# One gathered tile in 48 moves from GpSimd's indirect gather to SP's row-by-row copies

## What is computed

```python
N = emb.shape[0]
h = emb
acc = emb
for _ in range(LAYERS):
    h = jax.ops.segment_sum(adj_val[:, None] * h[adj_col], adj_row, num_segments=N)
    acc = acc + h
graph_item_embs = acc / (LAYERS + 1)
combined = graph_item_embs[items] + item_features[items]
...
scores = select @ _l2norm(graph_item_embs).T
```

## Time and profile before

| | us |
|---|---|
| median of 3 runs (lowest, highest) | 4309.99 (4309.81, 4310.87) |
| the profiled execution's own time | 4304.17 |
| its span in the profile | 4302.3 |
| sorting, until SP reads back the sorted lines | 0 to 738.3 |
| layer 0, GpSimd's first to last gather | 742.7 to 2302.0 |
| layer 1, GpSimd's first to last gather | 2334.4 to 3892.8 |
| GpSimd (POOL) busy in the whole span | 2982.2 (69%) |
| TensorE (PE) busy; VectorE (DVE) busy | 3380.7 (79%); 3127.0 (73%) |

### The profile page before, as it was taken

The page is one execution under the profiler, slowest core; times in us unless marked ns, Lnnn a source line. Parts: engine busy times, 40 slices in busy tenths (PEclk is TensorE's granted clock), DMA queues, the critical chain, the costliest instruction groups (busy, mean ns, idle before and its releaser), DMA issues. The chain is left out here.

```text
span 4302.3 us, 44283 instructions
## 1 busy us (share of the span) xinstructions
PE 3380.7 (79%) x9794; PEld 1811.7 (42%) x9794; DVE 3127.0 (73%) x7270; ACT 870.6 (20%) x3004; POOL 2982.2 (69%) x3071
## 2 busy tenths in 40 slices
PE   3899996787788877777876777777777777777888
PEld 2777774333333333333333333333333333334444
DVE  8999995777777777777775766667666776667555
ACT  0999996000000000000000000000000000007443
POOL 2477666777777777777775777777777777775760
PEclk8898887656665566666666767667676767766889
DMA  1000000221221221221125222222122221235693
GB/s 35 3 4 3 3 3 19 53 53 52 53 53 52 53 53 52 53 53 53 52 53 157 53 53 53 52 53 53 53 53 53 53 52 53 53 112 97 68 112 156
DMA packets 140407, 235.66 MB, mean 55 GB/s; under 512 B 56692, under 2 KB 84272, under 8 KB 140144
## 3 DMA queue, kind: packets, MB, share of 16 engines
q0 software_dynamic: 96288, 178.10, 19.1%
q1 hardware_dynamic: 41476, 55.61, 3.8%
q10 hardware_dynamic: 2508, 0.60, 0.1%
HBM read 193.16 MB, written 41.01 MB: 54 GB/s over the span
## 5 line engine op out<-in xcount | busy, mean ns | idle before, releaser
L1356 PE MATMUL bank<-ring 128*128 128x256 f32 x4992 | 2429.2, 604 | 692.5 <-DVE ring L1031 647.4
L1356 PEld LDWEIGHTS bank<-ring 128*128 128x128 f32 x4992 | 1120.9, 270 | 1977.5 <-DVE ring L1031 1941.4
L1031 DVE TENSOR_SCALAR ring<-bank,mlo,mval 128x256 f32<-128x256 f32 x2496 | 1353.2, 542 | 748.8 <-DMA ring<-table,cring 389.5
L516 POOL DMA_INDIRECT ring<-table,cring x1248 | 1178.5, 944 | 412.3 <-issue 379.9
L516 POOL DMA_INDIRECT ring<-in_L_rec_emb,cring x1248 | 1179.4, 945 | 384.4 <-issue 379.6
L1080 DVE TENSOR_TENSOR acc<-acc,bank 128x256 f32 x2496 | 1023.4, 410 | 172.1 <-issue 171.3
L602 ACT COPY mlo<-ring 128x24 f32 (+1 forms) x104 | 22.0, 211 | 2898.4 <-PE bank L1356 2895.4
L586 ACT ACTIVATE big<-big 128x68 f32<-128x68 bf16 x1764 | 558.0, 404 | 0.0
L1293 PE MATMUL bank<-big,ring 128*128 128x136 f32 x2352 | 441.3, 324 | 61.5 <-DVE ring L819 15.7
L486 POOL DMA_INDIRECT sorted_edges<-moved,block_to x313 | 399.7, 1277 | 101.9 <-issue 101.9
L1293 PEld LDWEIGHTS bank<-big,ring 128*128 128x128 f32 x2352 | 348.2, 211 | 152.7 <-ACT big L586 133.3
(11 more groups left out here) (209 smaller groups left out, 1620.7 us busy)
## 6 DMA issues: line engine op xcount, KB each, us to landing
scores<-stage SPq DMA_DIRECT2D x48, 512.0 KB, 2.6
ring<-in_L_rec_emb,cring POOLq DMA_INDIRECT x1248, 2.5
ring<-table,cring POOLq DMA_INDIRECT x1248, 2.5
table<-big SPq DMA_DIRECT2D x7, 896.0 KB, 8.4
combined<-ring SPq DMA_DIRECT2D x7, 896.0 KB, 7.5
sorted_edges<-moved,block_to POOLq DMA_INDIRECT x313
ring<-combined,sidi POOLq DMA_INDIRECT x200, 4.9
sorted_edges<-ring SPq DMA_DIRECT2D x1, 1248.0 KB, 4.4
```

The lines of the kernel that those rows point to most:

```text
L516: pool.indirect_dma_start(msg[:, s, :], None, source, bass.IndirectOffsetOnAxis(cring[:, s:s + 1], 0)).then_inc(s_g[s], 16)
L1031: dve.tensor_scalar(onehot[:, u % SR, :], bank[7][:, 0:BUCKET], mlo[:, u:u + 1], mval[:, u:u + 1], ALU.is_equal, ALU.mult).then_inc(s_S, 1)
L1356: pe.matmul(bank[u % PR][:, 0:BUCKET], msg[:, h * T + u, :], onehot[:, u % SR, :], start=True, stop=True).then_inc(s_mm[u % M], 1)
```

## The change

In both layers the last tile of each pair of rounds, slot 47 of `msg`, isn't gathered by GpSimd any more, except in the last pair. For the 25 other pairs SP copies its 128 rows one by one: SP loads 16 row numbers at a time into registers and issues 16 DMAs of one row each, with the source address from a register. The row numbers come from `own_col`, one partition wide, which DVE makes once from an extra read-back of the lines of these 25 tiles. SP starts on a pair's tile when the add of the same slot in the pair before is done (`s_acc[M - 1]`), waits for all 128 rows, clears their semaphore and raises `s_own_in`, for which DVE's one-hot of that slot waits. M becomes 4 in place of 6.

```diff
@@ constants @@
+    PAIRS = NST // 2 - 1
+    ROWS_AT_ONCE = 16
-    M = 6
+    M = 4
@@ semaphores @@
-        s_g = [sem(f"s_g{u}") for u in range(2 * T)]
+        s_g = [sem(f"s_g{u}") for u in range(2 * T - 1)]
@@ SP, behind the read-back of the sorted lines @@
+            sp.dma_start(own_lines.rearrange("o k s w -> o k (s w)"),
+                         lines[0:2 * T * PAIRS, :].rearrange("(k t) w -> t k w", t=2 * T)[2 * T - 1:2 * T]
+                         ).then_inc(s_lines, 16)
+
+            def last_of_pairs(layer, source):
+
+                sp.wait_ge(s_own, 2)
+                with sp.Fori(0, PAIRS) as i:
+                    sp.wait_ge(s_acc[M - 1], i * (2 * T // M) + (PER * layer + 1))
+                    for a in range(0, P, ROWS_AT_ONCE):
+                        _, cols = nc.values_load_multi_w_load_instructions(
+                            own_col[:, bass.ds(i * P + a, ROWS_AT_ONCE)], engines=[mybir.EngineType.SP],
+                            min_val=0, max_val=N - 1, skip_runtime_bounds_check_because=HELD)
+                        for p, col in enumerate(cols):
+                            sp.dma_start(msg[a + p:a + p + 1, 2 * T - 1, :], source[bass.ds(col, 1), :]).then_inc(s_one, 16)
+                    sp.wait_ge(s_one, 16 * P)
+                    sp.sem_clear(s_one)
+                    sp.sem_inc(s_own_in, 1)
+
+            last_of_pairs(0, emb)
@@ SP, behind the two loads of emb (413, 416 before) @@
+            last_of_pairs(1, table1)
@@ gather_step, GpSimd @@
-                for u in range(T):
+                for u in range(T if h == 0 or c == NST - 1 else T - 1):
@@
-                                            bass.IndirectOffsetOnAxis(cring[:, s:s + 1], 0)).then_inc(s_g[s], 16)
+                                            bass.IndirectOffsetOnAxis(cring[:, s:s + 1], 0)
+                                            ).then_inc(s_g[s] if s < 2 * T - 1 else s_late, 16)
@@ DVE, behind decode(T, NT, ...) @@
+            dve.wait_ge(s_lines, 16)
+            dve.tensor_copy(own_col.rearrange("o (k s) -> o k s", k=PAIRS), own_lines[:, :, :, 0]).then_inc(s_own, 1)
+            dve.wait_ge(s_own, 1)
+            dve.tensor_single_scalar(own_col, own_col, BUCKET.bit_length() - 1, ALU.arith_shift_right).then_inc(s_own, 1)
@@ one_hot, DVE @@
-                dve.wait_ge(s_g[u], 16 * ((NST // 2) * layer + it + 1))
+                if u < 2 * T - 1:
+                    dve.wait_ge(s_g[u], 16 * ((NST // 2) * layer + it + 1))
+                elif last:
+                    dve.wait_ge(s_late, 16 * (layer + 1))
+                else:
+                    dve.wait_ge(s_own_in, it + (PAIRS * layer + 1))
```

More of the change, by code:

```diff
@@ L93, in recommender_program @@
     TC = [T * (NST * n // 3) for n in range(4)]
+    HELD = "a column is held between 0 and N - 1, and an unused slot's is its tile's number, below NT <= N"
     FITS = "a tile's offset is 256 times the buckets that begin at or before it, less one: 0 to ROWS - 256"
@@ L151, in recommender_program @@
         sorted_rows = big[:, 0:-(-NT // P) * 2 * P].rearrange("p (m s w) -> p m s w", w=2, s=P)
+        at[0] = -(-NT // P) * 2 * P
+        own_lines = carve(big, PAIRS * 2 * P)[0:1, :].rearrange("o (k s w) -> o k s w", k=PAIRS, w=2)
+        assert at[0] <= ROWS
         at[0] = 0
@@ L209, in recommender_program @@
         block_at_l = carve(stage, NKL * P)
+        own_col = stage[0:1, 6 * D:6 * D + PAIRS * P].bitcast(I32)
+        assert 6 * D + PAIRS * P <= 4 * 512 * 2
         assert at[0] <= 4 * 512 * 2
@@ L317, in recommender_program @@
         s_iota = sem("s_iota")
-        s_g = [sem(f"s_g{u}") for u in range(2 * T)]
+        s_lines = sem("s_lines")
+        s_own = sem("s_own")
+        s_one = sem("s_one")
+        s_own_in = sem("s_own_in")
+        s_late = sem("s_late")
+        s_g = [sem(f"s_g{u}") for u in range(2 * T - 1)]
         s_S = sem("s_S")
@@ L1026, in _, with one_hot @@
             decode(T, NT, -(-NT // P))
-            def one_hot(layer, it, u):
-                dve.wait_ge(s_g[u], 16 * ((NST // 2) * layer + it + 1))
+            dve.wait_ge(s_lines, 16)
+            dve.tensor_copy(own_col.rearrange("o (k s) -> o k s", k=PAIRS), own_lines[:, :, :, 0]).then_inc(s_own, 1)
+            dve.wait_ge(s_own, 1)
+            dve.tensor_single_scalar(own_col, own_col, BUCKET.bit_length() - 1, ALU.arith_shift_right).then_inc(s_own, 1)
+            def one_hot(layer, it, u, last=False):
+                if u < 2 * T - 1:
[4 more added lines that the diff above has]
+                    dve.wait_ge(s_own_in, it + (PAIRS * layer + 1))
                 dve.tensor_scalar(onehot[:, u % SR, :], bank[7][:, 0:BUCKET], mlo[:, u:u + 1], mval[:, u:u + 1],
@@ L1084, in round_step @@
                     if not last or u + LEAD < T:
-                        one_hot(layer, it + (1 if h == 1 and u + LEAD >= T else 0), (h * T + u + LEAD) % (2 * T))
+                        one_hot(layer, it + (1 if h == 1 and u + LEAD >= T else 0), (h * T + u + LEAD) % (2 * T), last)
                 if layer == 0 and not (isinstance(c, int) and c >= L):
```

## The result

The changed kernel takes 4702.3 us (median of 4; 4694.1 to 4709.7) against 4309.9 before, a ratio of 1.0912 (95% interval 1.0898 to 1.0926). The forecast was slower, at 4442 us. The profiled execution took 4694.1 us.

What follows compares the result with a forecast made beforehand. GpSimd's gather step was taken as the bound; with SP setting the pace, layer 0 gains 61.2 us and layer 1 70.8, so 4304.2 + 132 = 4436, with 5.8 to the median 4442 us; 8-in-10 range 4238 to 4770.

Steps and rivals of the forecast that it cites:

- What bounds the kernel, and that SP takes over: Both layers run at GpSimd's gather step; SP's loop of 62.6 us a pair then sets the pace, against GpSimd's 58.7.
- G: Time from SP's release to its signal for one tile: 59.4 us, bounds 42 and 80.
- the issue: Issue of one single-row copy on SP: 0.29 us, between 0.17 and 0.42.
- register instruction and gaps: Per row on SP: one register instruction at 0.05 us and the gap between two issues at 0.045.
- A load of 16: SP's load of 16 row numbers into registers: 1.0 us, between 0.8 and 1.5; eight a tile, 8.0 us.
- The landing: SP's wait for its last row copy to land, with wait's end, clear and signal: 2.1 us a tile.
- The law of time over G: Each microsecond of G is worth 50 us; 56.8 gives no change, 55.5 or less gains the whole 62.5 us.
- Rival 1: SP keeps up and is hidden behind GpSimd, with a row at 0.355 us: 4248 us; chance 0.40.
- Rival 2: SP's issue costs 0.42 or 0.33 us, G 76 or 64.5: about 5270 or 4700 us; chance 0.20 above G = 64.
- Rival 3: SP's copies disturb GpSimd's gathers, step 1.28 us instead of 1.249: about 4323 us with SP hidden; chance 0.01.
- The loads' floor: Skill's floor of about 600 ns for SP's register loads: eight loads 4.8 us, G 56.2, time about 4282 us.
- Costed at nothing: Four semaphores, DVE's extra register instructions, the extra 25-row load, the moved features load and shared DMA engines were priced at zero.

Runs made afterwards that it cites:

- the 112-row run: Changed kernel with SP copying only rows 0 to 111 of its tiles, sums not the reference's: 4309.2 us beside 4307.4 for the kernel before.
- the split: Changed kernel with SP copying rows 0 to 95 and ACT rows 96 to 127: 4242.6 us against 4303.1 before; on the second kind of chip 6124 to 6203.
- 32-number loads: Changed kernel with 32 row numbers to a register load instead of 16: 4625.9 us against 4302.8 before; on the second kind of chip 6977 to 6995.

## Why the forecast had the sign and not the size

- *What bounds the kernel, and that SP takes over:* as forecast. DVE's wait for SP, GpSimd's wait for PE and SP without idle time were all named ahead.
- *The value of G:* the step that failed, a term that was mis-sized. The prediction said "G = 49.3 + 8.0 + 2.1 = 59.4 us". Measured: 51.7 + 10.1 + 1.0, and 1.3 in the slower rows, 64.1. By terms: the issue was put at 0.29 and took 0.22; register instruction and gaps were put at 0.095 and took 0.184, because a second register instruction stands there, and each of the three has a gap. The two errors nearly cancel, and leave + 2.4 us. A load of 16 was put at 1.0 and costs 1.26 with its surroundings, + 2.1; DVE's idle time of 1.53 us, from which it was scaled down, isn't what its load of 24 takes, which is 1.60 us. The landing was put 1.1 too high, and the slower rows weren't in the sum. Each microsecond counts 50 times, so 4.7 us are 235 of the 260 us missing; layer 1's dearer issues, 0.6 us in 25 pairs, are another 15.
- *The law of time over G,* "each microsecond of G is worth 50 us, G = 56.8 gives no change": right in three places. G = 56.8 gave 4309 us; G of 64.1 and 64.8 gives 4442 + 25 x (4.7 + 5.4) = 4695, measured 4702; SP hidden was to give 62.5 us and gave 60.5.
- *Rival 1,* SP keeps up, needed an issue of 0.26 us at the assumed gaps. The issue was even cheaper and the rival still failed, at the gaps and the loads. *Rival 2,* everything above G = 64, has the right time for a wrong reason: it wanted an issue of 0.33 or 0.42, and the issue took 0.22. Its 4700 is hit by chance. *Rival 3* is out on this kind of chip: GpSimd's gather takes 0.944 us with SP's copies and 0.945 without, and the 112-row run loses nothing.
- *The loads' floor.* The Trainium skill's "DMA: Bandwidth & Descriptors", section "Latency and other measured facts", gives a floor of about 600 ns. No load of these traces has fewer than 16 numbers, so they don't show it; from 1.14 us for 16 to 2.04 for 32 the number of registers decides. The same page says that the time to initiate a DMA is "usually small relative to the DMA itself" ("Issuing engines are not separate DMA queues"). For one copy the trace agrees, 0.22 us and at least 1.0 more to its landing; but 128 in a row are 28 us, and 51.7 with the instructions around them.
- *Costed at nothing:* four semaphores, the delayed start in layer 0 and the features load stayed free; the split contains all of them and comes within 2 us of the full gain. The jump back at the loop's end, 2.4 us, wasn't priced at all and is hidden in the 3.2 us.

## What to carry to other kernels

When work is moved from the engine that sets the pace to an idle one, compare the idle one's whole turn, with every small instruction, gap, load and landing, to the pace, and work out how much the total changes per unit of error; here 128 repeats and 50 turns turn 20 ns a row into 128 us. If the turn comes out near the limit, move less or share it: three quarters on SP and one quarter on ACT turned +9% into -1.4%. And a gain that rests on a queue of many short instructions should be measured on more than one chip.

## What the hardware showed that was not expected

- A DMA of one row with its address from a register is issued in 0.22 us on SP and on ACT, less than the 0.277 for 85 rows and 0.33 for 128. On SP it takes 0.404 from row to row with its two register instructions.
- A load into registers costs 0.24 us and 0.056 a number, by the sizes measured (1.14 for 16, 1.60 for 24, 2.04 for 32).
- Between chips the same kernel before differs by 14% (4303 to 4310 against 4917 to 4927 us), and the one with SP's long loop by much more (32-number loads: 4626 against 6990). The median of each instruction is the same, but while GpSimd gathers, SP's copies of one row follow each other in 1.29 us in place of 0.45; on the first kind the gathers make no such difference.
- A loop of 112 copies on SP brings five packets more on the instruction queue in each turn and takes 2.4 us to jump back, one of 96 copies 0.2 us and hardly a packet (351 against 110 to 113 in all).
